# ScalarE copies the tile before the one it exponentiates, with five f16 tiles, three f32 tiles and P times V four slots behind its scores

## The reference, cut to what matters

```python
q, k, v = x @ Wq + bq, ctx @ Wk + bk, ctx @ Wv + bv      # 16 heads of 32
scores = q @ k.T / sqrt(32); scores = where(j < i, scores, -1e30)
attn = softmax(scores); attn[:, :, 0, :] = 0
x = layer_norm(x + (attn @ v) @ Wo + bo)
out = layer_norm(x + relu(x @ W1 + b1) @ W2 + b2)
```

## Time and profile before

| | |
|---|---|
| median of 3 runs | 2654.29 us (2650.04 to 2656.82) |
| the profiled execution | 2651.14 us |
| its span | 2649.3 us |
| granted TensorE clock, mean | 0.989 |
| attention | to about 1180 us |
| feed-forward alone | from about 1260 us to the end |

### The profile page before, as it was taken

One profiled execution on the slowest core, in us unless ns is written; L12 is line 12 of the kernel. 1 busy time (PEld: TensorE's weight loads), 2 busy tenths in 40 slices (PEclk: granted clock), 3 DMA queues, 4 the chain that ended last, 5 costly groups with the idle time before them and its releaser, 6 DMA issues.

```text
span 2649.3 us, 62863 instructions
## 1 busy us (share of the span) xinstructions
PE 2498.2 (94%) x22664; PEld 1873.3 (71%) x22664; DVE 2116.9 (80%) x4886; ACT 1629.8 (62%) x2881; POOL 1585.5 (60%) x1721
## 2 busy tenths in 40 slices
PE   4899999999999999879999999999999999999998
PEld 1455555555555555557888888888888888888887
DVE  7999999999999999878767777767767676767675
ACT  2788889899899999886344444343444343444433
POOL 2677777777777777666455555555555555554543
PEclk9999999999999999989999999999999999999999
DMA  5344444443344443345232313222222222222220
GB/s 169 110 117 117 119 114 110 115 109 103 92 103 105 106 106 97 89 140 159 53 69 50 71 46 67 50 69 53 66 56 61 61 57 64 57 65 57 65 57 25
DMA packets 444456, 225.04 MB, mean 85 GB/s; under 512 B 302368, under 2 KB 388192, under 8 KB 444144
## 3 DMA queue, kind: packets, MB, share of 16 engines
q1 hardware_dynamic: 442544, 219.71, 32.5%
q10 hardware_dynamic: 1600, 1.31, 0.2%
HBM read 112.36 MB, written 57.69 MB: 64 GB/s over the span
## 4 chain that ended last, share of the span: by engine, by line
PE 63%; DVE 8%; SPq 8%; POOL 8%; issue 7%; DMA 4%; ACT 1%; ACTq 0%; DVEq 0%; POOLq 0%
PE h_ps L1646 23%; PE acc L1662 20%; POOL prob_lo L495 7%; PE front L1632 6%; PE lin_ps L934 5%; SPq L421 4%; PE max_ps L907 2%; PE st_ps L955 2%; DVE max_ps L886 2%; PE lin_ps L930 1%; PE o_ps L973 1%; SPq L458 1%; SPq L1065 1%; DMA heads<-stage 1%; PE st_ps L986 1%
## 5 line engine op out<-in xcount | busy, mean ns | idle before, releaser
L495 POOL TENSOR_TENSOR prob_lo<-probs,prob_hi 128x512 f16<-128x512 f32 (+1 forms) x768 | 797.8, 1047 | 335.2 <-ACT prob_hi L582 318.5
L1646 PE MATMUL h_ps<-x_halves,W 128*128 128x256 f16 x6144 | 756.2, 273 | 1.8 <-ACT hf L1431 1.7
L1662 PE MATMUL acc<-W,hs 128*128 128x256 f16 x5376 | 669.6, 273 | 0.3 <-DVE hs L1599 0.3
L1646 PEld LDWEIGHTS h_ps<-x_halves,W 128*128 128x128 f16 x6144 | 596.5, 98 | 87.5 <-issue 14.8
L1431 ACT ACTIVATE hf<-h_ps,b1s,scale_evac 128x256 f32<-128x256 f32 x512 | 284.9, 563 | 559.7 <-PE h_ps L1646 557.2
L1662 PEld LDWEIGHTS acc<-W,hs 128*128 128x128 f16 x5376 | 526.0, 98 | 61.4 <-DVE hs L1599 0.6
L1356 POOL TENSOR_TENSOR hf<-hf 128x256 f32<-128x256 f32 x256 | 243.4, 951 | 483.1 <-ACT hf L1431 482.7
L588 ACT ACTIVATE probs<-st_ps,exp_scale 128x512 f32<-128x512 f32 (+1 forms) x768 | 469.3, 611 | 98.2 <-PE st_ps L986 91.6
L886 DVE CUSTOM_DVE_ANT_0 max_ps<-max_ps,mask_q 128x256 f32<-128x256 f32 (+2 forms) x768 | 418.2, 560 | 47.1 <-PE max_ps L907 43.4
L582 ACT ACTIVATE prob_hi<-probs 128x512 f16<-128x512 f32 (+1 forms) x768 | 427.9, 557 | 23.0 <-issue 7.3
L1599 DVE TENSOR_TENSOR hs<-hf,hs 128x896 f16<-128x896 f32 x256 | 282.0, 1121 | 147.8 <-ACT hs L1420 147.7
(11 more groups left out here) (152 smaller groups left out, 3526.1 us busy)
## 6 DMA issues: line engine op xcount, KB each, us to landing
heads<-stage SPq DMA_DIRECT2D x748, 64.0 KB, 2.1
raw_c<-in_cT SPq DMA_DIRECT2D x64, 256.0 KB, 3.4
raw_x<-in_xT SPq DMA_DIRECT2D x64, 256.0 KB, 4.4
o_in<-ctx_rows SPq DMA_DIRECT2D x256, 64.0 KB, 2.5
x_in<-in_x SPq DMA_DIRECT2D x32, 512.0 KB, 4.0
x_rows<-x SPq DMA_DIRECT2D x64, 256.0 KB, 2.1
o_in<-x_rows SPq DMA_DIRECT2D x256, 64.0 KB, 2.4
out<-y SPq DMA_DIRECT2D x32, 512.0 KB, 3.0
```

Source lines behind the costliest of these rows:

```text
L495: pool.tensor_tensor(prob_lo[:, k % 4, 0:w], probs[:, k % PROBS, 0:w], prob_hi[:, k % 4, 0:w], ALU.subtract).then_inc(pl_done, 1)
L1646: last = pe.matmul(h_ps[:, f % 2, 0:T], W1[:, aw, j, f * P:(f + 1) * P], x1_halves[:, item.parity, aa, j, :], start=(j == 0 and m == 0), s ...
L1662: last = pe.matmul(acc_products[:, n, :], hs[:, p % HS, aa, n, :], W2[:, p, aw, n, :], start=(p == 0 and m == 0 and n % 2 == 0), stop=(p = ...
```

## The change

On ScalarE the two blocks change places: in a slot it first does the exp of tile k, then the copy of tile k-1. The f16 tiles `prob_hi` and `prob_lo` become five (`PARTS`, indexed by a running number, `part_at`), the f32 tiles `probs` three. P times V is four slots behind the scores, not three. `LIN` goes from 48 to 47, and with it all stages that count from it or are numbered with it, so that `PV_AT` stays at 93. The loads of the context stay in slots 0 to 3, and the weight scan and mix stay where they are.

```diff
-    LOAD = {"c": (0, 1, 2, 3), "x": (3, 6, 9, 12)}
-    LOOK = {"c": (9, 11), "x": (16, 20)}
-    TOPS = 21
-    SPREAD = 22
-    GATHER = 26
-    RANGE = 31
-    SPLIT = {"c": 36, "x": 48}
+    LOAD = {"c": (0, 1, 2, 3), "x": (2, 5, 8, 11)}
+    LOOK = {"c": (8, 10), "x": (15, 19)}
+    TOPS = 20
+    SPREAD = 21
+    GATHER = 25
+    RANGE = 30
+    SPLIT = {"c": 35, "x": 47}
     SPLIT_STEP = 3
-    LIN = 48
+    LIN = 47
...
-    PV_AT = ST_AT + 3
+    PV_AT = ST_AT + 4
...
-    PROBS = 4
+    PROBS, PARTS = 3, 5
...
+    def part_at(item, k):
+
+        return (SLOTS * item.n + k) % PARTS
...
-                    wait_for(pool, pv_done, SLOTS, item, k + 1 - 4)
-                    pool.tensor_tensor(prob_lo[:, k % 4, 0:w], probs[:, k % PROBS, 0:w],
-                                       prob_hi[:, k % 4, 0:w], ALU.subtract).then_inc(pl_done, 1)
+                    wait_for(pool, pv_done, SLOTS, item, k + 1 - PARTS)
+                    pool.tensor_tensor(prob_lo[:, part_at(item, k), 0:w], probs[:, k % PROBS, 0:w],
+                                       prob_hi[:, part_at(item, k), 0:w], ALU.subtract).then_inc(pl_done, 1)
...
-                for item, k in due(window, s, SLOTS, B, ST_AT + 1, SLOTS):
-                    w = ST_WIDTH[k % 3]
-                    wait_for(act, exp_done, SLOTS, item, k + 1)
-                    wait_for(act, pv_done, SLOTS, item, k + 1 - 4)
-                    act.activation(prob_hi[:, k % 4, 0:w], probs[:, k % PROBS, 0:w], ACT.Copy).then_inc(ph_done, 1)
...
+                for item, k in due(window, s, SLOTS, B, ST_AT + 1, SLOTS):
+                    w = ST_WIDTH[k % 3]
+                    wait_for(act, exp_done, SLOTS, item, k + 1)
+                    wait_for(act, pv_done, SLOTS, item, k + 1 - PARTS)
+                    act.activation(prob_hi[:, part_at(item, k), 0:w], probs[:, k % PROBS, 0:w], ACT.Copy).then_inc(ph_done, 1)
...
-FEED_AFTER = 46
+FEED_AFTER = 45
```

More of the change, by code:

```diff
@@ L238, in attention @@
         probs = sb("probs", [P, PROBS, S], F32)
-        prob_hi = sb("prob_hi", [P, 4, S], F16)
-        prob_lo = sb("prob_lo", [P, 4, S], F16)
+        prob_hi = sb("prob_hi", [P, PARTS, S], F16)
+        prob_lo = sb("prob_lo", [P, PARTS, S], F16)
         V = sb("V", [P, 2, QT, HEADS, VW], F16)
@@ L972, in values @@
                         v = V[:, item.parity, kt, h, :]
-                        pe.matmul(o[:, 0:2 * HD + 1], prob_hi[:, k % 4, col:col + P], v[:, 0:2 * HD + 1],
+                        pe.matmul(o[:, 0:2 * HD + 1], prob_hi[:, part_at(item, k), col:col + P], v[:, 0:2 * HD + 1],
                                   start=(k % 3 == 0 and q == 0), stop=False, skip_group_check=True)
-                        last = pe.matmul(o[:, HD:2 * HD + 1], prob_lo[:, k % 4, col:col + P],
+                        last = pe.matmul(o[:, HD:2 * HD + 1], prob_lo[:, part_at(item, k), col:col + P],
                                          v[:, HD:2 * HD + 1], start=False, stop=(c == 2),
```

## The result

The changed kernel takes **2714.86 us** (median of 4 runs, 2710.73 to 2718.8) against 2654.3 us in the same series: ratio 1.0232, 95% interval 1.0218 to 1.0246. The profiled execution took 2714.76 us, with a span of 2713.0 us, against 2649.3 us: 63.7 us more. The prediction was 2677 us, 2640 to 2700. The direction was right, the time lies 15 us above the range.

What follows compares the result with a forecast made beforehand. In the attention it saw three engines near 90% busy, with no fixed bound, and TensorE waiting for VectorE's maxima. Terms +19 + 6 + 3 - 3 + 1 = +26 on 2651.1 gave 2677 us, range 2640 to 2700.

Steps and rivals of the forecast that it cites:

- The load, +19: Second context chunk, now issued behind the 12 moves, makes VectorE wait at its first look in fourteen windows; +19 us.
- Passed on one for one: Step of the load term: what delays VectorE between slots 0 and 12 delays TensorE by as much; +19 us.
- ScalarE's order, 0 on the path and +3 for the emptying: ScalarE's exp ahead of copy: 58 us of its time saved, none on the path; emptying behind one more copy, +3 us.
- hidden behind TensorE and VectorE, on which ScalarE waits: Reason given for counting 0 of ScalarE's saved time: it waits on these two engines; 91.6 us for TensorE's scores.
- The mix and the rows, +6: Mixing windows: last addition some 1.9 us later, so the rows behind its store come later; 0.9 x 7 = +6 us.
- VectorE's redistribution -3: Heads' sums and normalisations on VectorE move one slot against the maxima, filling small idle spots; -3 us.
- P times V +1: End of the attention: the front of a sequence is one slot further ahead of P times V, once; +1 us.
- f32 tiles 0: Three f32 tiles: exp of tile k needs `prob_lo` of k-3; the loop fits by 0.3 us, so 0 us.
- the rival of the three f32 tiles: ScalarE waits for `prob_lo` in each window, not in the mix alone; +18 us on top, about 2695 us; chance 0.14.
- the period named among the signs, 67.2 us: Sign against the forecast: an unchanged period of 67.2 us with waits at the look means the waits are paid back.
- paid back: Rival: GpSimd runs on during VectorE's wait, so low parts behind it go faster; no change, about 2654 us; chance 0.18.
- faster: Rival: VectorE's new order takes a third of TensorE's 62.9 us for maxima; -12 us, about 2639 us; chance 0.18.

Runs made afterwards that it cites:

- a_load: The changed kernel with context chunks loaded in slots 0, 0, 1, 2, so the second is issued ahead of the moves of K and Q; 2686.66 us.
- r_tail: The changed kernel with ScalarE's copy ahead of the exp from window 15 on; 2711.26 us, the stretch behind the last table of tops 10.2 us shorter.
- s_mixwin: The changed kernel with ScalarE's copy ahead of the exp in windows 0 to 8 alone, those with the mix; 2700.4 us.
- c_order: The changed kernel with ScalarE's copy of tile k-1 ahead of the exp of tile k again, everywhere; 2686.8 us.
- f_both: The changed kernel with the copy ahead of the exp and the second context chunk issued ahead of the moves; 2657.04 us, ratio 1.0006.
- q_mix_first: The changed kernel with GpSimd's block of the mix ahead of its block of `prob_lo` in a slot; 2710.28 us.
- k_evac: The changed kernel with ScalarE's emptying of the projections between exp and copy, one slot earlier; 2705.65 us.
- g_swap: The kernel before with only ScalarE's two blocks exchanged, P times V still three slots behind and four tiles of each kind; 2725.6 us.

## Why the prediction was too low

- **The load, +19: the mechanism right, the term short.** The fourteen first looks wait 22.2 us, all looks 26.0. Of 23.5 us of waits that a_load removes, 18.8 come off TensorE's idle time, and 9.3 us more off its busy time. "Passed on one for one" is the step that failed, both ways: four fifths became idle time, and behind it TensorE's matmuls took longer, in the window shown at the lower clock. Measured 28, inside the bounds of 0 to 40. That the idle time is the predicted 19 is in part luck: the sum had 5.9 us of waits in the mixing windows and 13.1 in the others, the looks waited 9.6 and 12.7. The load landed 0.2 us sooner after its issue than before (3.0 for 3.2, means), and VectorE stood ready 0.3 us sooner (1.5 for 1.9), where the prediction kept the look's distance.
- **ScalarE's order, 0 on the path and +3 for the emptying: this step failed.** It measured 28. I had costed the gap between exp and copy, 58 us of ScalarE's time (39 came), and "hidden behind TensorE and VectorE, on which ScalarE waits" took that waiting for harmless. It was the reason for the loss: with the copy behind the exp, each wait for scores delays the copy, GpSimd's subtraction and all that stands behind that on GpSimd. Before, the copy of tile k-1 stood ahead of that wait. The traces show this link by link in the last tiles, and r_tail's stretch confirms it; in the mixing windows s_mixwin shows the cost, and the way it takes only in part.
- **The mix and the rows, +6: right in kind.** I had the last addition later behind one more exp and copy, and the rows behind it. The rows' wait grew by 9.1 us. It is a part of the order's cost, not a term beside it: in c_order it is 6.9 us, below the 11.0 of the kernel before.
- **VectorE's redistribution -3, P times V +1, f32 tiles 0: right in sum.** f_both puts all of them together within 0.16% of the kernel before; which of them cost or gave something isn't shown. ScalarE waits 7.9 us for `prob_lo` (1.7 before), where the rival of the three f32 tiles needed 18, so it fell.
- **Two slips that moved little.** A narrow copy takes 0.41 us in the trace, not 0.3, which makes the +3 a +4; and the period named among the signs, 67.2 us, is 67.0 by its own rows.
- **The rivals.** The waits weren't paid back. VectorE came to the looks early enough to wait 22 us there, so "faster" had no ground. No rival had the order as a loss, so the range ended too low.

How the order's 17.5 us in the mixing windows divide stays open. The late mix (q_mix_first, 9.7 in these windows) is the larger known part, the late emptying (k_evac, 3.5 in these windows, 585.1 us) the smaller; whether they overlap wasn't run, and the spread of some 5 us between kernels hides the rest.

## What to carry to other kernels

When two operations of an in-order engine change places, ask of each what it waits for and who is behind it: an operation with all its inputs ready belongs ahead of one that waits for another engine, even if that leaves a gap between dependent operations (28 us in this kernel, 72 in g_swap). Count a new wait of TensorE with what its busy time does afterwards, for which the runs give no fixed factor: taking the load's 18.8 us of idle time away gave 28, taking the order's 35.5 away gave 29. In a queue that is short of time an exchange helps where the transfer moved ahead is the one that is waited for and ready to go, as the load of a_load; the store, the rows and the moves only handed SyncE's delay to each other.

## What the hardware did that I had not expected

- **A small VectorE operation can take six times its time beside GpSimd.** The second step of the rows reads 16 elements per partition from each of two tiles in SBUF. First VectorE, then GpSimd, in the changed kernel:

```profile
844.99 0.18 DVE L825 SCALAR_TENSOR_TENSOR negmax_parts<-maxima,negmax_parts 128x16 f16<-128x16 f32 x1
875.58 1.08 DVE L825 SCALAR_TENSOR_TENSOR negmax_parts<-maxima,negmax_parts 128x16 f16<-128x16 f32 x1
```

```profile
846.88 3.08 POOL L499 TENSOR_TENSOR prob_lo<-probs,prob_hi 128x512 f16<-128x512 f32 x3 [1.95 <-ACT prob_hi L593]
874.35 2.27 POOL L499 TENSOR_TENSOR prob_lo<-probs,prob_hi 128x512 f16<-128x512 f32 x2 [0.75 <-ACT prob_hi L593]
```

  With GpSimd idle (until 846.88) it takes 0.18 us, beside a subtraction of GpSimd (874.35 to 876.62) 1.08, nearly the length of one such subtraction (1.16). Over the run the 64 of them went from 15.7 to 44.3 us in the change, and with the old order of ScalarE (c_order) they take 13.2. In the Trainium skill, "GPSIMD Engine Reference", "1. Specifications", it stands that GpSimd shares its SBUF interface with VectorE when that has two inputs there; these rows agree, and show that the price is that of GpSimd's operation and not in proportion to the small one's size.
- **A stall of a few microseconds can cost clock too.** In the rows above 2.51 us of waiting were followed by 3 us at a granted clock of 0.56, and 1.60 us, and in one place 3.03 us, by none. Of the 63.7 us of the result 14.0 are longer busy time, and the clock's part, estimated at 17, is of that size. It doesn't follow the idle time: c_order idles 35.5 us less than the changed kernel and has 78.5 us at the lower level, not fewer than its 75.
- **Order alone can cost 72 us** (g_swap, 2725.6 against 2654.0) in a kernel in which the engine whose order changes waits for others 92 us and becomes 28 us less busy (1629.8 to 1602.3).
